# Fused cross-attention and FFN on one core: the first loads split over SP's and ACT's DMA queues

## The reference, cut to what matters

```python
# x: (2, 2048, 512), ctx_768: (2, 77, 384), float32; 16 heads of 32
def xattn(query, key_value, Wq, bq, Wk, bk, Wv, bv, Wo, bo):
    q = (query @ Wq + bq).reshape(B, Nq, H, D).transpose(0, 2, 1, 3)
    k = (key_value @ Wk + bk).reshape(B, Nkv, H, D).transpose(0, 2, 1, 3)
    v = (key_value @ Wv + bv).reshape(B, Nkv, H, D).transpose(0, 2, 1, 3)
    attn = jnp.clip(jnp.einsum('bhqd,bhkd->bhqk', q, k) * scale, -CLAMP, CLAMP)
    attn = jax.nn.softmax(attn, axis=-1)
    return jnp.einsum('bhqk,bhkd->bqhd', attn, v).reshape(B, Nq, Cq) @ Wo + bo

def ffn(x, U1, V1, b1, U2, V2, b2):          # 512 -> 128 -> 2048 -> 128 -> 512
    H = jax.nn.gelu((x @ U1) @ V1 + b1)
    return (H @ U2) @ V2 + b2

x = x + xattn(layernorm(x), ctx_768, Wq, bq, Wk, bk, Wv, bv, Wo, bo)
x = x + ffn(layernorm(x), U1, V1, b1, U2, V2, b2)
```

## Time and profile before

| | |
|---|---|
| timed runs, median of 3 | 580.68 us (578.64 to 581.2) |
| profiled execution: its time | 577.34 us |
| profiled execution: its span | 575.5 us |
| PE busy | 554.8 us (96%) |
| DVE busy | 482.8 us (84%) |
| POOL busy | 366.6 us (64%) |
| ACT busy | 308.7 us (54%) |
| read from HBM, written to it | 32.49 MB, 16.78 MB |

### The profile page before, as it was taken

One profiled execution on the slowest core, in us unless ns is written; L12 is line 12 of the kernel. 1 busy time (PEld: TensorE's weight loads), 2 busy tenths in 40 slices (PEclk: granted clock), 3 DMA queues, 4 the chain that ended last, 5 costly groups with the idle time before them and its releaser, 6 DMA issues.

```text
span 575.5 us, 11999 instructions
## 1 busy us (share of the span) xinstructions
PE 554.8 (96%) x4804; PEld 464.2 (81%) x4804; DVE 482.8 (84%) x697; ACT 308.7 (54%) x510; POOL 366.6 (64%) x286
## 2 busy tenths in 40 slices
PE   8999999999999999999987997999999999999996
PEld 8787878888988898888865675888888888888884
DVE  4778989888988898888779968888979797978675
ACT  3464454445444545444456543757575766666652
POOL 2787767777676777677565564757566656565561
PEclk9999999999999999999989999999999999999999
DMA  8422353222323123220412431012121212101012
GB/s 311 163 79 75 110 202 112 93 70 71 101 92 112 54 77 112 92 75 20 148 56 74 129 112 72 0 75 73 74 73 67 81 56 91 57 19 56 18 61 86
DMA packets 25263, 50.36 MB, mean 87 GB/s; under 512 B 2936, under 2 KB 3064, under 8 KB 24824
## 3 DMA queue, kind: packets, MB, share of 16 engines
q1 hardware_dynamic: 24920, 49.07, 24.8%
q10 hardware_dynamic: 288, 0.52, 0.3%
HBM read 32.49 MB, written 16.78 MB: 86 GB/s over the span
## 4 chain that ended last, share of the span: by engine, by line
PE 78%; DVE 9%; DMA 6%; ACT 2%; POOL 2%; issue 2%; SPq 1%; POOLq 0%; DVEq 0%
PE bank L965 46%; PE ps_s L965 15%; PE bank L1040 5%; PE ps_s L1014 4%; PE bank L1056 4%; DMA xs<-in_x 4%; PE bank L1081 2%; PE bank L986 2%; DVE ss L748 1%; DVE smax L757 1%; DVE ssum L762 1%; DMA fw<-y_between 1%; DVE stats L687 1%; POOL ss L399 1%; DVE hs_r L824 1%
## 5 line engine op out<-in xcount | busy, mean ns | idle before, releaser
L471 POOL TENSOR_TENSOR hs_r<-ss,hs_r 128x512 fp32r<-128x512 f32 x63 | 90.3, 1434 | 90.1 <-ACT hs_r L667 89.5
L646 ACT ACTIVATE ss<-ps_s,once 128x512 f32<-128x512 f32 x128 | 87.9, 689 | 67.5 <-PE ps_s L965 64.0
L965 PE MATMUL ps_s<-p1t_r,v_r 128*128 128x512 f32 x384 | 112.2, 401 | 0.3 <-DVE p1t_r L813 0.3
L965 PE MATMUL bank<-hs_r,u_r 128*128 128x512 f32 x384 | 109.3, 393 | 0.7 <-DVE hs_r L824 0.7
L399 POOL TENSOR_TENSOR ss<-ss,smax 128x1232 f32<-128x1232 f32 x32 | 75.1, 2346 | 49.6 <-DVE smax L757 49.5
L965 PE MATMUL bank<-zt_r,wqo_r 128*128 128x256 f32 x768 | 98.7, 284 | 1.1 <-DVE zt_r L708 1.1
L965 PE MATMUL bank<-wqo_r,ot_r 128*128 128x512 f32 x384 | 98.9, 407 | 0.7 <-DVE ot_r L770 0.5
L965 PEld LDWEIGHTS bank<-zt_r,wqo_r 128*128 128x128 f32 x768 | 92.5, 188 | 2.8 <-DVE zt_r L708 1.3
L965 PEld LDWEIGHTS bank<-hs_r,u_r 128*128 128x128 f32 x384 | 72.0, 188 | 17.9 <-DVE hs_r L824 1.1
L965 PEld LDWEIGHTS bank<-wqo_r,ot_r 128*128 128x128 f32 x384 | 70.9, 191 | 16.6 <-DVE ot_r L770 0.9
L407 POOL TENSOR_TENSOR ss<-ss,rsum 128x1024 f32<-128x1024 f32 x32 | 61.5, 1922 | 35.7 <-DVE rsum L764 35.5
(11 more groups left out here) (86 smaller groups left out, 817.9 us busy)
## 6 DMA issues: line engine op xcount, KB each, us to landing
xs<-in_x SPq DMA_DIRECT2D x64, 256.0 KB, 3.5
y_between<-xs SPq DMA_DIRECT2D x32, 256.0 KB, 2.0
xs<-y_between SPq DMA_DIRECT2D x4, 1024.0 KB, 5.9
fw<-y_between SPq DMA_DIRECT2D x4, 1024.0 KB, 5.6
out<-xs SPq DMA_DIRECT2D x16, 256.0 KB, 2.0
out<-fw SPq DMA_DIRECT2D x16, 256.0 KB, 2.0
ss<-in_wq SPq DMA_DIRECT2D x2, 512.0 KB, 8.1
xs<-in_Wo SPq DMA_DIRECT2D x1, 1024.0 KB, 9.5
```

What stands on the lines that cost most here:

```text
L471: pool.tensor_tensor(hs[:, c % 4, 1, :], hg[:, c % 4, :], hs[:, c % 4, 0, :].bitcast(F32), ALU.subtract)\
L646: act.activation(hg[:, c % 4, :], ps_s[:, c % 4, :], ACT.Gelu_apprx_tanh, bias=b1_c[:, c:c + 1]).then_inc(h_gelu, 1)
L965: mm = pe.matmul(ps, lhs(a), rhs(c), start=first and i == 0, stop=last and i == len(PASSES) - 1)
```

## The change

Wk and the second half of Wq are issued by ACT, as the first two instructions of its list. SP issues x of block 0, ctx, the first half of Wq, and then the rest in the old order. Sizes, buffers, semaphores and the readers' waits stay.

```diff
             load_x(0, 0)
             sp.dma_start(once[:, UB * D - KC * B * KV:], ctx_bias).then_inc(in_ctx, 16)
-            sp.dma_start(wk_f, wk).then_inc(in_wk, 16)
-            for half in range(2):
-                sp.dma_start(wq_f[half], wq[half]).then_inc(in_wq[half], 16)
+            sp.dma_start(wq_f[0], wq[0]).then_inc(in_wq[0], 16)
             load_x(0, 1)
             sp.dma_start(wo_f, wo).then_inc(in_wo, 16)
             sp.dma_start(wv_f, wv).then_inc(in_wv, 16)
...
         @block.scalar
         def _(act):
+            act.dma_start(wk_f, wk).then_inc(in_wk, 16)
+            act.dma_start(wq_f[1], wq[1]).then_inc(in_wq[1], 16)
```

## The result

The changed kernel takes 581.38 us (median of 22 runs) against 579.49 us for the kernel before on the same chips; the ratio is 1.0041, 95% interval 1.0025 to 1.0057. That is 2.4 us more (0.0041 x 579.49), from 1.4 to 3.3 us. The forecast was 1.3 us more, on the side that was measured; by the bound of 0.5% it counts as no change. The 581.38 us measured lie in the range given (579.7 to 584.2) and 0.6 us from the forecast of 582.0, but that is partly luck: it was built on a kernel before of 580.68 us (three executions), which over 22 executions has 579.49, and on a loss that was too small.

What follows compares the result with a forecast made beforehand. TensorE's stream of matrix products was taken to bound the kernel, the edit moving only its start. 2.1 us later at K's projection less 0.8 given back is +1.3 on 580.68 us: 582.0 us, range 579.7 to 584.2.

Steps and rivals of the forecast that it cites:

- The order of bytes: First loads: x of block 0 shares the DMA engines packet by packet, complete at 7.3 us, z 3.0 us later.
- Rival (2): First loads: queues change over in larger groups, x landed at 6.3 us; +0.3 us, 581.0 us; chance 0.12.
- Rival (3): First loads: nothing happens to x, since ACT's first transfer starts late; 580.7 us; chance 0.14.
- rival (4): Block 2 of x lands early while x of block 0 isn't held up; faster, 579.9 us; chance 0.07.
- Wk, K: Start of K's projection: Wk no longer waited for, 0.91 us given back; K starts 2.1 us later (1.5 to 2.8).
- Wq: Q's projection: both halves of Wq ready before TensorE asks, covered by 1.1 us and 0.7 us.
- The second wait: VectorE's wait for block 2 of x before the first clip goes, giving back 0.80 us; +1.3 us at 25.36 us.
- The stream has no further wait for a load: After 25.36 us: TensorE's stream waits for no further load, so it runs as before, 1.3 us later.
- Rival (1): TensorE's idle time before z of block 0: the clock falls, costing 1.5 us, 583.5 us; chance 0.24.

Runs made afterwards that it cites:

- e4: Changed kernel with the load of x of block 6 issued ahead of the FFN weights; 579.04 us, ratio 1.0011 to the kernel before.
- e3: Kernel before with the load of x of block 6 issued ahead of the FFN weights; 576.34 us, ratio 0.9957.
- e5: Changed kernel with x of block 6 loaded ahead of the FFN weights and 52 warming transposes in place of 32; 577.93 us, ratio 0.9961.
- e1: Changed kernel run once more without an edit; 580.4 us, ratio 1.0038 to the kernel before.
- e12: Kernel before run once more without an edit; one execution, 581.76 us.
- e8: Kernel before with six loads on SP's queue in the order in which the changed kernel ends them; one execution, 582.9 us.
- e6: Kernel before with x of block 6 loaded ahead of the FFN weights and x of block 2 ahead of Wv; 576.47 us, ratio 0.9937.
- e7: e6 with transposes of the identity added in the second FFN block, at a place without a gap; 576.98 us, ratio 0.9937.
- e2: Changed kernel with ACT's two loads waiting until the first half of x has landed; 584.97 us, ratio 1.0106 to the kernel before.
- e13: e6 with 22 transposes of the identity in TensorE's idle time near 346 us; 575.04 us, ratio 0.993.

## Why the prediction was right, and where its sizes were off

**The order of bytes.** Right. x complete: 7.3 us forecast, 7.14, 7.25 and 7.25 us (e4) measured. The time came out by luck, since two terms were wrong and cancelled: I took the case in which ACT's packets begin later, with 1.57 MB ahead, at 305 GB/s. They did begin later (27 packets of x by 2.0 us, none of ACT's), but ACT's queue made up for it: by 7.0 us it had moved 1.29 of its 1.31 MB. So nearly all 1.83 MB came first, at 372 GB/s from 2 to 7 us. Rival (2), larger groups, is refuted for groups of a whole load: by 4.28 us no engine had ended either load, and 209 packets of both were through. Rival (3) is refuted by the first half of x at 5.13 us, and rival (4) falls with it, since it needed x of block 0 not to be held up.

**Wk, K.** 0.91 us given back, as written. But K started 1.58 us later, not 2.1. In before, TensorE's warming transposes had ended only as the turn began at 7.19 us, when half of z had been there for a while, and this slack of some 0.3 us I had not seen. 1.58 is within the 1.5 to 2.8 given.

**Wq.** Covered, as written: the low part of the second half was ready at 16.0 us (13.60 + 2.40), TensorE got to it at 16.75.

**The second wait.** The mechanism was right: no idle time before block 2, the clip started by the scores (block 2 was there by 18.93 us, not at 19.6). The term was mis-sized by being taken from one execution. It gave 1.45 - 0.74 = 0.71 us against the first profile of before; against the second profile the start at Q of block 1 is 26.10 - 24.73 = 1.37 us, with nearly nothing given back. e3 agrees with the first (25.31 us). So the start costs 0.7 to 1.4 us in single profiles in which the clock held (0.9 from e3 to e4, 1.0 from e3 to e5), about the 1.3 forecast.

**"The stream has no further wait for a load."** Wrong. It has one near 79 us, before x of block 6, in both kernels, 2.1 to 2.8 or 3.7 to 4.0 us long. I hadn't read the timeline that far. The first profile of after showed 1.5 us more there, and 2.2 us more near 350 us; from these two profiles alone one would blame the change for 4.5 us. e1 and e12 show that the long form of the wait comes and goes in either kernel.

**The clock.** Rival (1) came true in part: in one of the four profiles with a gap of 1.7 to 3.0 us there (e1; not in after, e4 and e8). It cost 1.5 us there, as priced. e5, without executions in the upper part of the spread, shows that it matters. A second place the prediction did not price at all, although had a part of it: the gap near 346 us. Behind it the clock fell, for 3.4 or 6.8 us, in all four profiles with the changed start (after, e1, e4, e5) and in none of the three with the old one (before, e12, e3). Near 296 us, where a fall cost some 0.1 us in e3, it fell in all three with the old start and in one of the four with the changed one (after). e3 and e4 price this at 1.1 us. What decides the place stays open: e6 and e7, without the change, have the fall near 350 us, and e8, with the late start, has not.

**The sum.** 1.3 us forecast (0.7 to 2.0), 2.4 (1.4 to 3.3) measured. The forecast has no term for anything behind 25 us. The start is 0.7 to 1.4 of what was measured. Some 1.1 more is what the place of the low clock costs in e3 and e4, and together these are 1.8 to 2.5 us; but this rests on seven profiles, and is not shown for the mean of the executions. It fits that at the same mean clock of 0.997 the changed kernel of e1 (579.98 us, 7 executions) and the kernel before beside it (577.87, 17) are 2.1 us apart: the length of the low clock is not it there, its place may be. The long form of the wait near 79 us may also be more frequent in one kernel than in the other, and the profiles don't tell. The interval's lower end needs no rest.

## What to carry to other kernels

Here the second DMA queue did little for the rate by itself (380 GB/s against 359 on one queue in nearly the same order); it changed the order of the bytes. In these runs the packets of the two queues ran about one for one, so that the load with the larger rows takes the larger share. Put what the first chain of work needs alone at the head, and ask what every later load, on either queue, does to it. Before a difference of a few us is read out of two profiles, profile each kernel twice: waits for loads and the clock after a gap move by more than that in an unchanged kernel. And look where the clock was low, not only for how long: the same 3.4 us cost some 0.1 us in one place and 1.1 us in another.

## What the runs showed of the hardware

- The rate of the first loads depends on their order: 305, 266 and 281 GB/s from 2 to 8 us in the kernel before (first profile, e12, e3), 359 with the same queue and another order (e8, one profile), 375 to 380 in the four profiles of the changed kernel with two queues (after, e1, e4, e5).
- A load issued on the idle queue did not start at once: in e2 none of its packets ran for 3.6 us after its issue at 3.36 us, while the other queue worked off what it had issued earlier. bv in the earlier trace rows is of this kind: issued at 11.58 us, it had no packet before 15.0 us.
- An idle time of TensorE of 2.43 us (e1) was followed by 3.4 us at the lower level of 1.2 GHz, one of 2.76 us (after) was not; one of 3.20 us near 346 us was not in before, and one of 3.23 us was in after, for 6.8 us. The length of the gap alone doesn't decide. With transposes of the identity in the gap the clock stayed up in both profiles that had them there (e5, e13); so it did in some profiles without them.
